# Expert tiles in pairs: a new order of TensorE's work in a sine-attention and mixture-of-experts block

## The reference

```
x = x + Attention(LayerNorm(x))      # 16 heads of 8, sin(30 * q.k / sqrt(8)) in place of a softmax
x = x + MoE(LayerNorm(x))
# MoE: expert(x) = (silu(x Wg^T) * (x Wu^T)) Wd^T, hidden width 256
# one shared expert for all tokens, plus the two best of 8 routed experts,
# each weighted by its sigmoid score
```

## Time and profile before

| | |
|---|---|
| median of 3 runs | 473.99 us (473.74 to 475.28) |
| profiled execution, first to last instruction | 471.0 us |
| what lies beside the span, by the median | 3.0 us |
| TensorE, ScalarE, VectorE, GpSimd busy | 90%, 74%, 65%, 51% |
| mean granted TensorE clock | 0.991 |

### The profile page before, as it was taken

One profiled execution on the slowest core, in us unless ns is written; L12 is line 12 of the kernel. 1 busy time (PEld: TensorE's weight loads), 2 busy tenths in 40 slices (PEclk: granted clock), 3 DMA queues, 4 the chain that ended last, 5 costly groups with the idle time before them and its releaser, 6 DMA issues.

```text
span 471.0 us, 13125 instructions
## 1 busy us (share of the span) xinstructions
PE 421.8 (90%) x4648; PEld 225.2 (48%) x4648; DVE 305.0 (65%) x1058; ACT 348.0 (74%) x551; POOL 239.5 (51%) x322
## 2 busy tenths in 40 slices
PE   2899989999989999989999999889999989799872
PEld 1422233333423354444544545444544678789871
DVE  6877585644735355748674648684557578488994
ACT  1577978978888987868778886778788476676640
POOL 5351541300287141315865886227684787568851
PEclk9999999999999999999999999999999999999987
DMA  5037679727218514672264626862112256541220
GB/s 170 4 104 211 134 239 292 185 92 201 48 43 267 122 33 132 163 153 57 74 186 139 143 67 183 183 137 63 52 42 58 74 120 131 135 121 46 71 63 29
DMA packets 82479, 56.11 MB, mean 119 GB/s; under 512 B 29040, under 2 KB 76784, under 8 KB 82416
## 3 DMA queue, kind: packets, MB, share of 16 engines
q1 hardware_dynamic: 78112, 47.74, 38.9%
q0 software_dynamic: 3584, 7.35, 6.0%
q10 hardware_dynamic: 720, 0.20, 0.2%
HBM read 22.62 MB, written 27.13 MB: 106 GB/s over the span
## 4 chain that ended last, share of the span: by engine, by line
PE 57%; DVE 15%; issue 10%; ACT 7%; POOL 5%; DMA 4%; SPq 1%; ACTq 0%; DVEq 0%; POOLq 0%
PE o_ps L651 17%; PE score L638 9%; ACT attn L888 5%; PE g_ps L760 4%; PE g_ps L762 4%; PE g_ps L761 4%; PE d_ps L778 3%; DVE hid L1220 3%; DVE x_all L1263 2%; PE r_ps L664 2%; ACT gate L909 2%; DMA y_back<-in_wd 2%; POOL y_back L1455 2%; PE r_ps L614 2%; PE d_ps L780 2%
## 5 line engine op out<-in xcount | busy, mean ns | idle before, releaser
L888 ACT ACTIVATE attn<-score 128x1024 f32<-128x1024 f32 x256 | 248.2, 1024 | 26.7 <-PE score L638 26.2
L1436 POOL TENSOR_TENSOR hid_lo<-hid,hid_hi 128x256 f16<-128x256 f32 x108 | 75.9, 703 | 137.3 <-DVE hid_hi L1227 124.3
L651 PE MATMUL o_ps<-attn,vals 128*32 128x512 f32 x1024 | 136.4, 605 | 0.8 <-ACT o_t L895 0.5
L638 PE MATMUL score<-queries,keys 64*128 64x512 f16 x512 | 82.5, 383 | 9.5 <-ACT attn L888 8.0
L1220 DVE SCALAR_TENSOR_TENSOR hid<-g_ps,gate 128x256 f32<-128x256 f32 x102 | 43.2, 423 | 54.1 <-ACT gate L909 53.0
L909 ACT ACTIVATE gate<-g_ps 128x256 f32<-128x256 f32 x102 | 39.2, 384 | 45.4 <-PE g_ps L762 43.6
L778 PEld LDWEIGHTS d_ps<-w_hi,hid_hi 128*128 128x128 f16 x198 | 19.3, 97 | 59.6 <-issue 53.0
L760 PE MATMUL g_ps<-xt,w_hi 128*128 128x128 f16 x248 | 44.8, 220 | 1.1 <-DVE hid L1220 1.0
L761 PE MATMUL g_ps<-xt,w_hi 128*128 128x128 f16 x248 | 44.8, 220 | 0.0
L762 PE MATMUL g_ps<-xt,w_lo 128*128 128x128 f16 x248 | 44.7, 219 | 0.0
L778 PE MATMUL d_ps<-w_hi,hid_hi 128*128 (+1 forms) x198 | 39.1, 223 | 5.1 <-issue 2.8
(11 more groups left out here) (220 smaller groups left out, 985.7 us busy)
## 6 DMA issues: line engine op xcount, KB each, us to landing
y_sorted<-y_sb SPq DMA_DIRECT2D x84, 64.0 KB
q_four<-q_parts SPq DMA_DIRECT2D x14, 256.0 KB
queries<-q_four SPq DMA_DIRECT2D x14, 256.0 KB
k_four<-k_minus SPq DMA_DIRECT2D x14, 256.0 KB
keys<-k_four SPq DMA_DIRECT2D x14, 256.0 KB
x_sorted<-zeros SPq DMA_DIRECT2D x2, 1472.0 KB, 8.5
queries<-q_three SPq DMA_DIRECT2D x14, 192.0 KB
keys<-k_three SPq DMA_DIRECT2D x14, 192.0 KB
```

The lines of the kernel that those rows point to most:

```text
L638: mm = pe.matmul(score[h][:, i, :], keys[b % 2][rows, 2 * j + h, kt * P:(kt + 1) * P], queries[b % 2][rows, 2 * j + h, :], start=True, sto ...
L651: mm = pe.matmul(o_ps[32 * i:32 * i + 32, :], vals[b % 2][:, kt, h:h + 32], attn[k % RING][:, i, :], start=(k == 0), stop=(k == UNITS - 1))
L888: act.activation(attn[k % RING][:, 2 * (u % 2):2 * (u % 2) + 2, :], score[u % 2][:, :, :], ACT.Sin, scale=SIN_SCALE).then_inc(sined, 1)
L1436: pool.tensor_tensor(hid_lo[i % HB][:, :], hid[i % HR][:, :], hid_hi[i % HB][:, :], ALU.subtract).then_inc(lo_by_pool, 1)
```

## The change

Tiles go in pairs (`DUOS`). Their matrices are 128x512 where they were 128x256, the engines' operations on them twice as wide. Gate/up matmuls of shared and dense pairs take 256 columns. In the main part a pair goes every fourth slot, at slots that are 2 modulo 4; values go two units at a time at slots that are 0 modulo 4. The down part follows eight slots after its gate/up part. One tensor `tile_ps` of two banks takes gate in bank 0 and up in bank 1; the down result of the main part goes into bank 1 too. Row work is put at other slots. A combination is spread over five slots. Buffers: `hid` 2 (of a pair) for 5 (of a tile), `hid_hi` and `hid_lo` 4 for 8, `y_sb` 3 for 6.

```diff
-LAG = 4
-LAST_SUMS = {0: 14, 2: 15}
+QUAD = 4
+TURN = 2
-S_XT1, S_COPYX1, S_Q, S_SCALEQ, S_K, S_SCALEK, S_V = 1, 2, 3, 4, 8, 9, 11
+S_XT1, S_OUT, S_Q, S_K, S_V, S_XT2, S_ROUTE, S_PREFIX = 2, 2, 6, 6, 10, 14, 14, 22
+S_COPYO, S_COPYX1, S_SCALEQ, S_SCALEK, S_COPYX2 = 2, 3, 7, 8, 15
...
-    for a in range(SLOTS + 1, TAIL, 2):
+    for a in range(SLOTS + TURN, TAIL, QUAD):
...
 def down_slots():
+        a = a + 6 if a >= TAIL else min(a + 2 * QUAD, TAIL + 4)
...
 # TensorE
-                    if s % 2 == 0:
-                        scores(b, s)
-                        scores(b, s + 1)
-                    if s % 2 == 0 and s >= LAG:
-                        sum_values(b, (s - LAG) // 2)
+                    scores(b, s)
+                    scores(b, s + 1)
+                if s == 0 and 1 <= b <= ROWS and a <= TAIL:
+                    sum_values(b - 1, UNITS - 2)
+                    sum_values(b - 1, UNITS - 1)
+                elif b < ROWS and s % QUAD == 0 and s:
+                    sum_values(b, s // 2 - 2)
+                    sum_values(b, s // 2 - 1)
...
 # gate_up: the up half waits for the read of the last down result
+                    if k == CH:
+                        done = sum(D_SLOT[i] <= GU_SLOT[d] for i in range(min(d, D_MAIN)))
+                        if done and (d < GU_MAIN or d == GU_MAIN + SETS - 1):
+                            wait_read(pe, done - 1)
...
 # VectorE
-                for g, row in combines_at(a):
-                    combine(g, row, 0)
-                for g, row in combines_at(a - 1):
-                    combine(g, row, 1)
+                for t in range(TT):
+                    for g, row in combines_at(a - t):
+                        combine(g, row, t, 0)
+                    for g, row in combines_at(a - t - 1):
+                        combine(g, row, t, 1)
```

More of the change, by code:

```diff
@@ L727, in _, with look_ahead @@
             placed = set()
-            def look_ahead(i, pieces):
-                if i < NT and TILES[i][0] == SPARSE and TILES[i][1:3] in place_of and (i, pieces) not in placed:
-                    placed.add((i, pieces))
+            def look_ahead(d, pieces):
+                if d < ND and DUOS[d][0] == SPARSE:
+                    _, g, first, _, n = DUOS[d]
                     for k in pieces:
-                        for part in (w_hi, w_lo):
-                            pe.lower_ap(piece(i, part[k]), for_matmul_weights=pieces == GU_PIECES)
@@ L737, in gate_up @@
-            def gate_up(i):
-                kind, row, t, e = TILES[i]
+                        for m in range(n):
+                            if (g, first + m) in place_of and (d, k, m) not in placed:
+                                placed.add((d, k, m))
+                                for part in (w_hi, w_lo):
+                                    pe.lower_ap(piece(d, m, part[k]), for_matmul_weights=k in GU_PIECES)
+            def gate_up(d):
+                kind, row, t, e, n = DUOS[d]
@@ new lines, in gate_up, with down @@
+                mm.then_inc(gu_done, 1)
+            def down(d):
+                kind, row, t, e, n = DUOS[d]
+                if D_HOME[d] == "up":
+                    pe.wait_ge(hid_ready, sum(a < D_SLOT[d] for a in GU_SLOT))
+                elif D_HOME[d] == "o":
+                    pe.wait_ge(o_ready, ROWS)
+                else:
+                    pe.wait_ge(logit_ready, ROWS)
+                if D_HOME[d] in D_HOME[:d]:
+                    wait_read(pe, d - 1 - D_HOME[:d][::-1].index(D_HOME[d]))
+                wait_lo(pe, d)
+                look_ahead(d, D_PIECES)
+                for m in range(n):
+                    here = d_bank(d)[:, m * DM:(m + 1) * DM]
+                    for c in range(CH):
+                        hi, lo = (half[d % HB][:, c, m * P:(m + 1) * P] for half in (hid_hi, hid_lo))
+                        hi_part, lo_part = piece(d, m, w_hi[2 * CH + c]), piece(d, m, w_lo[2 * CH + c])
+                        pe.matmul(here, hi, hi_part, start=(c == 0), stop=False)
+                        pe.matmul(here, lo, hi_part, start=False, stop=False)
+                        mm = pe.matmul(here, hi, lo_part, start=False, stop=(c == CH - 1))
@@ L810, in _ @@
             pe.wait_ge(ld_wo, 16)
-            for a in range(END + 1):
+            for a in range(0, END + 1, 2):
                 b, s = divmod(a, SLOTS)
@@ L842, in _ @@
                         project_q(b + 1, r_ps[:, :])
-                    if ahead == S_K:
-                        project_k(b + 1, r_ps[:, :])
                     if ahead == S_V:
@@ new lines, in read_down @@
+                if kind == SHARED:
+                    dve.wait_ge(x1_done, row + 1)
+                    dve.scalar_tensor_tensor(out=pair, in0=here, scalar=DOWN_UNSCALE, in1=pair, op0=ALU.mult, op1=ALU.add).then_inc(d_read, 1)
+                    return
+                dve.wait_ge(weight_ready, ROWS)
+                wait_read(dve, DUOS.index((FULL, row, t, e - 1, 2) if e else (SHARED, row, t, None, 2)))
+                for m in range(2):
+                    ins = dve.scalar_tensor_tensor(out=x_tile(row, t + m), in0=here[:, m * DM:(m + 1) * DM], scalar=weight[len(ROUTE_GROUPS) % 2][:, t + m, e:e + 1],
+                                                   in1=x_tile(row, t + m), op0=ALU.mult, op1=ALU.add)
```

488 lines of the change are left out of this document (247 added, 241 removed).

## The result

| | before | after |
|---|---|---|
| median of 4 runs | 473.87 us | 494.42 us (490.67 to 497.32) |
| ratio | | 1.044 (95%: 1.040 to 1.048) |
| span of the profiled execution | 471.0 us | 493.2 us |
| TensorE, ScalarE, VectorE, GpSimd busy | 90, 74, 65, 51% | 84, 68, 57, 46% |
| mean granted TensorE clock | 0.991 | 0.969 |

Executions more than 1.5% above the fastest of the same kernel are left out of every ratio in this document, and are kept in the medians in us.

What follows compares the result with a forecast made beforehand. ScalarE paces slots 0 to 127, TensorE bounds 128 to 253, and TensorE waits for VectorE in the tail. Terms +10.7 - 3.3 - 5.2 = +2.2, span 473.2; 3.0 more for the median: 476 us, range 464 to 488.

Steps and rivals of the forecast that it cites:

- Two values follow each other without a gap: Slots 128 to 253: two values units in a row take 1.90 us, with no 0.09 us gap between them.
- Where ScalarE sets the pace: Slots 0 to 127: four slots take 4.64 us, before 2 x 1.84 to 1.9; ScalarE idles 0.9 us each time.
- the second pieces in `r_ps`: Slots 96 to 127: second projection of a step waits for ScalarE's copy of the first; 2.3, 1.7, 1.6 us over.
- The `xn` chain ahead of the shared bank's read: Slots 28 to 30, rows 3 to 5: aggregation, power and xn delay reading slot 30's down result, 1.7 us each.
- the shares: Row 4: an extra 1.1 us on the delay of slot 30's read.
- the bank's read: Slots 128 to 253: up part waits for VectorE's read of the down result, just covered where VectorE is free.
- the 4 us "that I can't place": Slots 128 to 253: 4 us of unlocated TensorE waits, added to 10.0 placed, making 14 against 9.5 idle before.
- the placed ones: Slots 128 to 253: waits from late reads, shares, spread combinations, ScalarE's copies and places, 10.0 us in sum.
- clearly slower: Slots 128 to 253: shared bank's read late as often as now, 27 of 47, by 0.75 us; 485 us, chance 0.17.
- Nothing for both; if SP were late, the loads it feeds would cost what the 1.5 above holds: SP's and GpSimd's queues cost nothing; late SP loads would fit the tail's 1.5 us for loads.
- SP's and GpSimd's queues: Fewer stores hold SP less, and a group's first scatter waits for a load issued some 30 slots earlier; no cost.
- gathers with a 1.28 hid_lo, 1.0: Tail, slots 254 on: gathers together with a hid_lo of 1.28 us make 1.0 us of waits.

Runs made afterwards that it cites:

- e7_order: Changed kernel with row 0's row work two slots earlier, placements later, queries' loads ahead of keys' stores, key steps moved: 523.0 us, ratio 1.060.
- f4_late: g1_all with placements, stores and loads left as in the changed kernel, so keys come late: 507.6 us, ratio 1.022.
- g2_nolook: g1_all with the register reads back four slots ahead of use, as in the changed kernel: 512.2 us, ratio 1.041.
- g1_all: Changed kernel with keys' trip reordered, row 3 copies on VectorE, one combination earlier, register reads two slots ahead, first norm earlier: 503.6 us, ratio 1.022.
- e6_early: Changed kernel with the combination of group 1's last row five slots earlier, still spread: 491.0 us, ratio 1.037.

## Why the prediction was wrong

*Right.* Two values follow each other without a gap (1.86 from the first to the next kind, 1.90 forecast). Where ScalarE sets the pace four slots take 4.61 us (4.64 forecast). In row 3 the second pieces in `r_ps` waited 2.30, 1.34 and 2.18 us, 5.8 together (the forecast had 2.3, 1.7 and 1.6 over the free time, 5.6), in rows 1 and 2 0.8 to 0.9, and once 1.50. The `xn` chain ahead of the shared bank's read cost 1.36, 2.33 and 1.41 us, 5.1 with the shares (forecast 6.2). The work between slots 128 and 253 fell by 5.8 us (178.5 for 184.3; 7.8 forecast, and some 1.6 of the difference is half clock), and the bank's read was no general wait: all waits of gate/up parts for reads were 6.2 us. Part of the near hit in this stretch is luck: besides the waits behind register reads TensorE idled 7.0 us there, where 14 were forecast, so the 4 us "that I can't place" and 3 of the placed ones were not there, and they hid most of the term that was missing. The rival "clearly slower" gave 485, the nearest of the four, but by a mechanism that the trace does not show.

*The step that failed first* is "Nothing for both; if SP were late, the loads it feeds would cost what the 1.5 above holds". The sum moved the row work on TensorE, and never followed its products through VectorE, SP's queue and memory to slot 32. That is 4.05 + 1.89 us of waits, less the 0.9 of ScalarE's pace in each, about 2.6 of half clock, and 0.6 of a longer wait for `xn_t`: the +3.1 and +4.3 of slots 20 to 63. The cause is shown by e7_order, where both waits went when the stores began earlier and the queries' loads went ahead; f4_late sizes it at 6.5 us of slots 20 to 95, 4.4 after the price of the shift.

*Between 128 and 253* a term was missing altogether: the register reads, 9.9 us of exposed waits, 6.8 to 8.5 us by g2_nolook. They are in the program's order before and after and in none of the sums. The trace of before has 2.8 us of such waits in this stretch, ahead of L778 (1.26 and 0.99 us, at slots 145 and 209, and two of 0.3), each behind such a read, so the new order added 7.1. The Trainium skill (TensorE: Matmul & The Clock Gate, Architectural detail: the array is 16× 32×32, not 1× 128×128) gives the depth of TensorE's queue as 64. No run here shows the depth, but the traces agree that work is queued ahead of the array and that it hides the reads: a read behind 0.54 us of scores was followed by an idle time of its own length or 0.25 us less, and in g1_all seven of the nine reads between slots 119 and 253, behind two values, by none.

*In the tail* "SP's and GpSimd's queues" again, and "gathers with a 1.28 hid_lo, 1.0": that term measured 5.17 us and 6.7 us of half clock, which cost about 2.9 more. The forecast took the gain of a spread combination (the waits for L1250's reads are gone) and not its price, that GpSimd waits for its end. With that one moved, in e6_early, the tail is 99.8 us, 5.5 less than the 105.3 of before; the forecast of 5.2 less would have held.

*The clock* stood in no sum. Its share is in the first and third of these, in 1.4 us at slot 112, behind the wait of 2.18 us for ScalarE's copy, and in the 3.3 us from 244.6.

## What to carry to other kernels

Where a change moves a producer, follow its product to the last consumer, through each queue and memory, and count the slots that are left at the fastest pace of that stretch. Where it moves work away from ahead of a sequencer's own instruction (here a register read), ask how much queued work still hides it: such waits show as idle time without a releaser, or are put down to the engine that finished last. And spreading a burst delays its end: name who waits for the end, not only who suffers the burst.
